# Moving small passes, splits and blank rows of an attention kernel between engines

## The reference, cut to what matters

```python
x = x + attention0(layernorm(x), ctx)        # scores / sqrt(8) + position bias, mask, softmax
x = x + ffn(layernorm(x))                    # low-rank, 512 wide, gelu
x = x + attention1(layernorm(x), ctx)        # softmax without bias
x = x + moe(layernorm(x))                    # 16 experts of 64, top 8 by tanh gate, silu, one shared
```

## Time and profile before

| what | us |
|---|---|
| median of 3 runs | 200.42 (199.63 to 200.68) |
| profiled execution, its own time | 201.42 |
| its span | 199.6 |
| PE busy | 169.8 (85%) |
| DVE busy | 148.3 (74%) |
| ACT busy | 133.3 (67%) |
| POOL busy | 91.1 (46%) |

### The profile page before, as it was taken

One profiled execution on the slowest core, in us unless ns is written; L12 is line 12 of the kernel. 1 busy time (PEld: TensorE's weight loads), 2 busy tenths in 40 slices (PEclk: granted clock), 3 DMA queues, 4 the chain that ended last, 5 costly groups with the idle time before them and its releaser, 6 DMA issues.

```text
span 199.6 us, 4779 instructions
## 1 busy us (share of the span) xinstructions
PE 169.8 (85%) x1609; PEld 120.5 (60%) x1609; DVE 148.3 (74%) x651; ACT 133.3 (67%) x289; POOL 91.1 (46%) x110
## 2 busy tenths in 40 slices
PE   0548269998979699989789679989999999999994
PEld 0325145667658366655656356857766767869783
DVE  5390369898588967998686979898986944989461
ACT  3265046999999879998988978572687674344120
POOL 8159999989789968964230533001010020110000
PEclk9999958999999979999999979999999999999999
DMA  5255796012323862000303302300010001000000
GB/s 134 80 116 130 176 252 140 1 39 72 92 56 97 218 211 68 13 0 4 82 6 78 82 8 62 96 8 0 2 32 2 0 5 30 0 2 0 29 1 26
DMA packets 21880, 12.22 MB, mean 61 GB/s; under 512 B 3120, under 2 KB 21232, under 8 KB 21856
## 3 DMA queue, kind: packets, MB, share of 16 engines
q1 hardware_dynamic: 19776, 10.68, 21.3%
q10 hardware_dynamic: 2080, 1.24, 2.4%
HBM read 4.98 MB, written 0.54 MB: 28 GB/s over the span
## 4 chain that ended last, share of the span: by engine, by line
PE 67%; ACT 12%; DVE 10%; issue 4%; POOL 4%; DMA 2%; SPq 1%; DVEq 0%; ACTq 0%
PE bank L460 17%; PE bank L489 10%; PE bank L403 8%; PE bank L359 6%; PE bank L374 4%; PE bank L343 3%; PE bank L439 3%; PE bank L429 3%; ACT pt L1401 3%; DVE es L887 3%; ACT xn L1349 2%; PE bank L413 2%; PE bank L476 2%; PE bank L420 2%; PE bank L349 2%
## 5 line engine op out<-in xcount | busy, mean ns | idle before, releaser
L887 DVE CUSTOM_DVE_ANT_0 es<-bank,biasq 128x128 f32<-128x128 f32 x128 | 28.1, 284 | 7.8 <-PE bank L359 7.6
L1735 POOL TENSOR_TENSOR es<-es,mx 128x512 f32<-128x512 f32 x32 | 32.7, 1044 | 0.7 <-DVE mx L887 0.6
L1713 POOL TENSOR_TENSOR rstd<-ve,half 128x2 f32<-128x2 f32 x16 | 11.2, 700 | 44.3 <-DVE ve L872 43.9
L1455 ACT ACTIVATE gth<-bank 128x256 f32<-128x256 f32 (+1 forms) x36 | 13.2, 382 | 21.8 <-PE bank L460 17.1
L403 PE MATMUL bank<-pt,va 128*32 128x128 f32 x512 | 26.1, 288 | 1.5 <-ACT pt L1401 0.8
L374 PE MATMUL bank<-ident,es 128*128 128x128 f32 x128 | 19.6, 294 | 4.7 <-ACT es L1395 4.1
L460 PE MATMUL bank<-xT,wg 128*128 128x256 f32 (+1 forms) x72 | 22.9, 399 | 0.1
L893 DVE TENSOR_REDUCE mx<-bank 128x4 f32<-128x512 f32 x32 | 20.5, 679 | 2.8 <-PE bank L359 2.7
L1395 ACT ACTIVATE es<-es 128x512 f32<-128x512 f32 x32 | 19.1, 630 | 5.1 <-POOL es L1735 5.1
L460 PE MATMUL bank<-xT,wu 128*128 128x256 f32 (+1 forms) x72 | 21.4, 379 | 0.0
L489 PE MATMUL bank<-wd,hT 128*128 128x128 f32 x128 | 21.2, 291 | 0.2 <-DVE hT L1010 0.2
(11 more groups left out here) (141 smaller groups left out, 343.1 us busy)
## 6 DMA issues: line engine op xcount, KB each, us to landing
k0st<-k0p SPq DMA_DIRECT2D x24, 64.0 KB, 2.1
k1st<-k1p SPq DMA_DIRECT2D x24, 64.0 KB, 2.1
q1st<-q1p SPq DMA_DIRECT2D x24, 64.0 KB, 2.0
q0st<-q0p SPq DMA_DIRECT2D x21, 64.0 KB, 2.1
biasq<-rel_bias_scratch SPq DMA_DIRECT2D x4, 256.0 KB, 4.5
wg<-in_wg SPq DMA_DIRECT2D x1, 544.0 KB, 6.0
wu<-in_wu SPq DMA_DIRECT2D x1, 544.0 KB, 6.3
x<-in_x SPq DMA_DIRECT2D x4, 128.0 KB, 4.5
```

The source lines that it names most:

```text
L887: ins = dve.tensor_tensor_reduce(es[:, b, h], src[:, s * SEQ:(s + 1) * SEQ], biasq[:, h], 1.0, 3.0e38, ALU.add, ALU.min, mx[:, 0, p, b, h: ...
L1455: act.activation(gth[0:rows, n % GATES], src[0:rows, 0:TOK], ACT.Silu).then_inc(nth("gth", n), 1)
L1735: pool.tensor_tensor(es[:, b, h], es[:, b, h], mx[:, 0, p, b, h].unsqueeze(2).broadcast_to([128, 4, SEQ]), ALU.subtract).then_inc(nth(f"le ...
```

## The change

Four things are done together.

1. `ve` and `nmr` of each layer norm, the four passes of `split_max` and the four of the combine split go from DVE to POOL. `nmr` is now one pass for each sequence. `split_max` and `router_parts` on POOL have the passes of before, behind waits on DVE's results and on their own.
2. The 15 splits: ACT casts part 0 from PSUM, PE adds the product of the negated identity with part 0 to the bank, ACT casts part 1, PE subtracts that, ACT casts part 2 and frees the bank. `first_rest`, `last_part` and `middle` are gone. The score's scale goes into the query weights (`scale_queries`, DVE), and DVE makes the negated identity.
3. The blank rows of q1 and k1 are filled by two transfers a stack from a small tile (`clear_rows`, SP; 12 in all), with -1 in k1, as the maxima are no longer negated.
4. All five orders and the bank numbers are new. In ACT's order the loads of weights stand behind all splits of pair 1 and ahead of the first exponential.

The core of the diff, with the first calls of PE, ACT, POOL and SP:

```diff
 
+            if first(j, p):
+                if part == 0:
+                    freed(q, f"{j}.{p}")
+                else:
+                    new(q, "q0_first", part) and q.wait_ge(sem("q0_first"), part)
+            elif part < 2:
+                new(q, f"{j}_part{part}", turn(j, p) + 1) and q.wait_ge(sem(f"{j}_part{part}"), turn(j, p) + 1)
+            else:
+                freed(q, f"{j}.{p}")
             if part == 0:
...
+        def clear_rows(q, j, i):
+
+            new(q, "blanks", 2) and q.wait_ge(sem("blanks"), 2)
+            for n in range(PRODS, DK):
+                load(q, stacks[j][i][n:128:DK], blanks[:, 1 if j == "k1" else 0].unsqueeze(1).broadcast_to([2 * DK, HALF, TOK]), f"{j}st{i}_in")
+
         def stacked(eng, j, p):
...
+            def less_part(j, p, part):
+
+                new(pe, "identb", 2) and pe.wait_ge(sem("identb"), 2)
+                new(pe, f"{j}_part{part}", turn(j, p) + 1) and pe.wait_ge(sem(f"{j}_part{part}"), turn(j, p) + 1)
+                pe.matmul(filling(f"{j}.{p}")[:, 0:TOK], minusb[:], parts[j][p % SPLITS[j]][:, part], start=False, stop=True,
+                          skip_group_check=True).then_inc(nth(f"{j}_less{part}", turn(j, p)), 1)
 
...
@@ -527,333 +549,363 @@
             rel_bias(0)
             front_turned(0, 1)
             project("q0", 0, 2)
-            project("k0", 0, 3)
-            project("k1", 0, 4)
+            project("k1", 0, 3)
+            project("k0", 0, 4)
+            less_part("k1", 0, 0)
+            less_part("k0", 0, 0)
+            less_part("k1", 0, 1)
             front_turned(1, 5)
-            project("k0", 1, 6)
-            project("q0", 1, 7)
+            less_part("k0", 0, 1)
+            project("q0", 1, 6)
+            project("k0", 1, 7)
             project("k1", 1, 0)
-            scores0(0, 0, 0, 1, 3)
-            scores0(0, 0, 2, 2, 4)
-            scores0(0, 1, 0, 5, 6)
+            less_part("q0", 1, 0)
+            less_part("k0", 1, 0)
+            less_part("q0", 1, 1)
+            less_part("k0", 1, 1)
+            scores0(0, 0, 0, 1, 2)
+            scores0(0, 0, 2, 5, 3)
+            scores0(0, 1, 0, 4, 6)
             scores0(0, 1, 2, 7, 1)
-            weights_turned(0, 0, 0, 3)
-            value_rows(0, 0, 3)
+            value_rows(0, 0, 2)
             value_rows(0, 1, 2)
-            values(0, 0, 0, 0, 3)
-            weights_turned(0, 0, 1, 2)
-            value_bias_out(4)
-            weights_turned(0, 0, 2, 5)
+            weights_turned(0, 0, 0, 2)
+            weights_turned(0, 0, 1, 5)
+            value_bias_out(2)
...
-                new(dve, f"mv{n}", 2 * p + 2) and dve.wait_ge(sem(f"mv{n}"), 2 * p + 2)
-                dve.tensor_scalar(ve[:, n, p], mv[:, n, p, :, 1], LN_EPS, None, ALU.add).then_inc(nth(f"ve{n}", p), 1)
-
-            def shift(n, p):
-
-                new(dve, f"rstd{n}", p + 1) and dve.wait_ge(sem(f"rstd{n}"), p + 1)
-                dve.scalar_tensor_tensor(nmr[:, n, p], mv[:, n, p, :, 0], -1.0, rstd[:, n, p], ALU.mult, ALU.mult).then_inc(nth(f"shift{n}", p), 1)
 
             def add_bias(p, b, c):
 
...
+            def scale_queries():
+                new(dve, "wqk_in", 16) and dve.wait_ge(sem("wqk_in"), 16)
+                for l in range(2):
+                    dve.tensor_scalar(wqk[:, l, 0], wqk[:, l, 0], SCALE if l else -SCALE, None, ALU.mult).then_inc(nth("wq_scaled", l), 1)
 
...
-            def evict(j, p):
+            def split(j, p, part):
 
...
-                if p >= SPLITS[j]:
+                l, to = int(j[1]), parts[j][p % SPLITS[j]][:, part]
+                if part == 0 and p >= SPLITS[j]:
                     stacked(act, j, p - SPLITS[j])
-                i = p % SPLITS[j]
-                l = int(j[1])
+                if part:
+                    new(act, f"{j}_less{part - 1}", turn(j, p) + 1) and act.wait_ge(sem(f"{j}_less{part - 1}"), turn(j, p) + 1)
                 if j[0] == "q":
                     new(act, "bqs", 2) and act.wait_ge(sem("bqs"), 2)
-                    bias, scale = bqs[:, l:l + 1], SCALE if l else -SCALE
+                    bias = bqs[:, l:l + 1]
                 else:
                     new(act, "bqk_in", 16) and act.wait_ge(sem("bqk_in"), 16)
-                    bias, scale = bqk[:, 2 * l + 1:2 * l + 2], 1.0
-                act.activation(parts[j][i][:, 0], src, ACT.Identity, bias=bias, scale=scale)
-                free(act.activation(whole[j][i][:], src, ACT.Identity, bias=bias, scale=scale), f"{j}.{p}")
-
-            def middle(j, p):
-                new(act, f"{j}_rest", turn(j, p) + 1) and act.wait_ge(sem(f"{j}_rest"), turn(j, p) + 1)
-                i = p % SPLITS[j]
-                act.activation(parts[j][i][:, 1], whole[j][i][:], ACT.Copy).then_inc(nth(f"{j}_mid", turn(j, p)), 1)
+                    bias = bqk[:, 2 * l + 1:2 * l + 2]
+                ins = act.activation(to, src, ACT.Identity, bias=bias)
+                if part < 2:
+                    ins.then_inc(nth(f"{j}_part{part}", turn(j, p)), 1)
+                else:
+                    free(ins, f"{j}.{p}")
 
...
             copy_front(0)
-            evict("k0", 0)
-            evict("k1", 0)
-            middle("k0", 0)
+            split("k1", 0, 0)
+            split("k0", 0, 0)
+            split("k1", 0, 1)
             normalize(0, 1)
-            middle("k1", 0)
             stack(act, "q0", 1, 0)
+            stack(act, "q0", 2, 0)
+            split("k0", 0, 1)
             copy_front(1)
-            stack(act, "q0", 2, 0)
-            evict("k0", 1)
-            evict("q0", 1)
-            middle("k0", 1)
-            middle("q0", 1)
+            split("k1", 0, 2)
+            split("k0", 0, 2)
+            split("q0", 1, 0)
+            split("k0", 1, 0)
+            split("q0", 1, 1)
+            split("k0", 1, 1)
+            split("q0", 1, 2)
+            split("k0", 1, 2)
+            load_wv(act)
             load_wo(act)
-            load_wv(act)
+            load_rows(act)
             load_bv(act)
             load_ffn(act)
-            load_rows(act)
             load_gate(act)
+            load_b1(act)
+            copy_values(0, 0)
             weights0(0, 0, 0)
-            load_b1(act)
             weights0(0, 0, 1)
+            copy_values(0, 1)
             copy_weights(0, 0, 0)
...
+
                 new(pool, "half", 1) and pool.wait_ge(sem("half"), 1)
+                new(pool, f"mv{n}", 2 * p + 2) and pool.wait_ge(sem(f"mv{n}"), 2 * p + 2)
+                pool.tensor_scalar(ve[:, n, p], mv[:, n, p, :, 1], LN_EPS, 1.0, ALU.add, ALU.mult).then_inc(nth(f"ve{n}", p), 1)
                 new(pool, f"ve{n}", p + 1) and pool.wait_ge(sem(f"ve{n}"), p + 1)
                 pool.tensor_tensor(rstd[:, n, p], ve[:, n, p], half[:, 0:2], ALU.pow).then_inc(nth(f"rstd{n}", p), 1)
+                new(pool, f"rstd{n}", p + 1) and pool.wait_ge(sem(f"rstd{n}"), p + 1)
+                for b in range(2):
+                    pool.tensor_scalar(nmr[:, n, p, b:b + 1], mv[:, n, p, b, 0:1], rstd[:, n, p, b:b + 1], -1.0,
+                                       ALU.mult, ALU.mult).then_inc(nth(f"shift{n}", 2 * p + b), 1)
 
             def residual(n, p):
...
+                new(pool, "nm_pads", 1) and pool.wait_ge(sem("nm_pads"), 1)
+                if p:
+                    read(pool, f"nm.{p - 1}{b}")
+                for c in range(4):
+                    freed(pool, f"S1.{p}{b}{c}")
+                to = nm[:, b]
+                src, rest = (t.rearrange("p (hh hp) -> p hh hp", hh=2) for t in (mx[:, 1, p, b], mr[:, p, b]))
+                pool.tensor_copy(to[:, 0], src).then_inc(nth(f"nm_a{b}", p), 1)
+                new(pool, f"nm_a{b}", p + 1) and pool.wait_ge(sem(f"nm_a{b}"), p + 1)
+                pool.tensor_tensor(rest, src, to[:, 0], ALU.subtract).then_inc(nth(f"nm_b{b}", p), 1)
+                new(pool, f"nm_b{b}", p + 1) and pool.wait_ge(sem(f"nm_b{b}"), p + 1)
+                pool.tensor_copy(to[:, 1], rest).then_inc(nth(f"nm_c{b}", p), 1)
+                new(pool, f"nm_c{b}", p + 1) and pool.wait_ge(sem(f"nm_c{b}"), p + 1)
+                pool.tensor_tensor(to[:, 2], rest, to[:, 1], ALU.subtract).then_inc(nth(f"nm{b}", p), 1)
+
+            def router_parts(p):
+
...
+
             def clear(j, i):
-                pool.memset(stacks[j][i][:], 1.0 if j == "k1" else 0.0).then_inc(nth(f"{j}_clear", i), 1)
+                pool.memset(stacks[j][i][:], 0.0).then_inc(nth(f"{j}_clear", i), 1)
...
             value_ones()
-            clear("q1", 0)
-            first_rest("k0", 1)
-            first_rest("q0", 1)
-            last_part("k0", 1)
-            clear("q1", 1)
-            clear("q1", 2)
+            clear_blanks()
             less_least(0, 0, 0)
             less_least(0, 0, 1)
-            last_part("q0", 1)
-            clear("k1", 0)
             less_least(0, 0, 2)
-            clear("k1", 1)
             less_least(0, 0, 3)
             less_least(0, 1, 0)
...
```

(112 more changed lines are left out.)

976 lines of the change are left out of this document (446 added, 530 removed).

## The result

The changed kernel takes 193.52 us (four runs, 192.59 to 194.42), the kernel before 200.22 (four runs beside them). The ratio is 0.967, 95% interval 0.961 to 0.972, so 6.7 us are gone. Forecast were 2.9. The profiled execution took 193.92 us, its span is 192.1.

What follows compares the result with a forecast made beforehand. TensorE, busy 169.8 of 199.6 us, bounds the kernel, with ScalarE the other full engine in the middle. Idle -5.3, clock -1.6 and products +4.0 sum to -2.9, giving 197.5 us, own range 195.5 to 199.4, whole range 193.3 to 202.8.

Steps and rivals of the forecast that it cites:

- Orders redrawn: All engine orders: fewer table loads and calls moved past the first experts, moved work counted once, priced at nothing.
- Products, +4.0: TensorE's 30 subtracting products: the 22 outside the opening at 0.18 us each cost 4.0 us, from 3.1 to 5.9.
- Middle, -5.3, and clock, -1.6: From 30 to 122 us: half of TensorE's 10.7 us idle returns, and half of 3.2 us clock loss around gaps.
- GpSimd, "no bound": GpSimd's total busy time goes from 91.1 to 87.9 us with tiny passes in and subtractions and memsets out: no bound.
- the splits' relief, "nothing": Splits in PSUM: ScalarE keeps three passes per projection at 0.48 us each, so nothing is gained.
- Opening, 0: First 30 us: hand walk to first scores at 21.3 and exponential at 27.5; nothing taken, ends -2 to +2 us.
- Tiny passes, 0.3 each: 96 tiny passes moved from VectorE to GpSimd cost 0.3 us each there, 28.8 us in all.
- rival 4: GpSimd's tiny passes cost 0.7 us each, lengthening norm and split_max chains: +4.5 us, 204.9; chance 0.07.
- Tail, nothing: From 122 to 197 us, mostly experts: TensorE idles only 0.9 us, so nothing unless its own work changes.
- Rival 3: Experts in the tail: VectorE is a hidden bound, and relief saves 3.6 us more over 36 calls: 193.9; chance 0.15.
- Rival 1: Middle, 30 to 122: ScalarE, busy 83.4 of 92 us, holds it at 92; 199.5 to 201, say 200.2; chance 0.20.
- Rival 2: At the 22 later subtracting products TensorE waits 0.4 us for ScalarE's splits: 201.9 at half, 206.3 at all; chance 0.15.

Runs made afterwards that it cites:

- e7: Kernel before with tiny passes on GpSimd and splits in PSUM, old orders but for the places of touched calls, memsets as before: 201.20 us, ratio 1.003.
- e11: Changed kernel with the router and first seven expert calls of pair 0 put back behind the scores and last queries of pairs 2 and 3: 200.25 us, ratio 0.994.
- e12: Changed kernel, same parts, all five orders drawn anew with more experts of pairs 0 and 1 ahead of 122 us: 194.25 us, ratio 0.966.
- e13: Changed kernel, same parts, a second new set of orders, nearer to the change's own: 198.29 us, ratio 0.987.
- e4: Changed kernel's orders and banks with tiny passes, splits and memsets all put back as before: 209.59 us, ratio 1.037.
- e8: Changed kernel with a second, all-zero product behind each of the 30 subtracting products: 195.01 us, ratio 0.971.
- e10: Changed kernel with 30 unconnected GpSimd passes added at the places of the old subtractions: 200.37 us, ratio 0.997.
- e2: Changed kernel with the splits back over SBUF, GpSimd subtracting in 30 passes, the 30 products gone: 202.01 us, ratio 1.003.
- e1: Changed kernel with the tiny passes back on VectorE, all else as changed: 200.85 us, ratio 0.998.
- e3: Changed kernel with blank rows of q1 and k1 cleared by six GpSimd memsets again, no blank-row transfers: 193.66 us, ratio 0.964.
- e5: Kernel before with only the tiny passes moved to GpSimd, orders otherwise as before: 203.19 us, ratio 1.014.

## Why the prediction was wrong

The direction and the place (TensorE's idle middle) were right, the size wasn't: -6.7 against -2.9. In the profiles PE's idle time fell by 9.8 us where the forecast's term had 5.3, and its busy time rose by 2.3 where its terms had 2.4 (-1.6 and +4.0). So the miss lies in the idle time. By the steps:

1. *The step that failed: "Orders redrawn", put at nothing ("moved work, counted once").* The forecast gave the whole gain of the middle to the two parts, whatever the orders. With both parts in the old orders nothing is gained: 201.20, ratio 1.003, and PE idles 10.2 us from 30 to 122 as before (e7), where the forecast, which has no term for the orders, asks for 197.5. One move of the new orders, the first experts ahead of the last scores, is worth 5.5 us with all parts unchanged (e11): it is what stands in the place where PE waited at 115. Two other orders of the same parts are 4.2 us apart (e12, e13). But the orders aren't the gain by themselves: with the old parts they lose 7.4 us against before (e4). The gain belongs to neither alone. How it divides, the runs don't tell: an undone part also leaves an order that doesn't fit it, and in the old orders I chose the places.
2. *Products, +4.0.* I divided a busy time by a count (5.9 / 32). Added a second time, thirty of them cost the kernel about 1 us (e8). With about 1 for 4 the sum would have been -5.9 and 194.5, near the result, but for the wrong reason, as 1 shows. The busy time doesn't settle what the first thirty cost: they show 0.28 to 0.31 us each, 9.0 in sum, and the engine's total rose by 2.3 while about 2 us less went to the lower clock (mean granted clock 0.964 over 199.6 us before, 0.973 over 192.1 now). Part of them must fall where PE would have stood idle.
3. *Middle, -5.3, and clock, -1.6.* 6.2 us of idle came back. That the stretch 75 to 97 can't give was right: PE idles 2.5 us there, 2.3 before. The clock loss around both gaps went whole (3.2 by the earlier trace rows), not half, but the opening ran at 0.87 against 0.92, 1.5 us more lost; the net of about 2 is near the 1.6 by that accident.
4. *GpSimd, "no bound", and the splits' relief, "nothing".* I compared totals (91.1, then 87.9) and looked at ScalarE and TensorE alone. GpSimd was busy 52.3 of 60 us between 30 and 90, with 0.7 us of idle ahead of its `less_least` calls, and I didn't read that column. In the new orders its time has a price: 19 us more of it cost 6.1 (e10), the old splits 7.3 (e2). That it held the kernel before isn't shown, and three runs speak against it, if not each by itself: relieved in the old orders it gave nothing (e7); relieved further in the new ones, the kernel was as slow as before (e1); and 9.4 us more of its busy time, by the memsets, cost nothing (e3).
5. *Opening, 0.* PE idles 2.7 us less. Its wait for the first `xn` went from 2.6 us to 0.4, and is 0.4 in e1 too, with the tiny passes on VectorE, so it isn't theirs. The walk was late at each step: first scores at 20.2 (21.3 forecast), load issues 0.49 each (0.56), exponential at 25.7 (27.5). The memsets were rightly called hidden (e3).
6. *Tiny passes, 0.3 each.* 0.20 to 0.29, 22.1 us for 96 where I had 28.8. One chain, at 64.06: `ve` to the end of `nmr` 1.6 us, of the 2.0 forecast to `xn`. Whether a dear pass (rival 4) was a danger is answered: no. The Trainium skill prefers VectorE for elementwise work and calls GpSimd slower at two inputs (GPSIMD Engine Reference, Engine selection). Pass by pass the trace agrees in direction, by less: the last pass of the combine split takes 0.24 us on GpSimd, 0.19 on VectorE. For the kernel the move cost 2.7 us in the old orders (e5), with GpSimd at 55.1 of those 60 us, and undoing it cost 6.4 in the new ones (e1).
7. *Tail, nothing.* 0.9 us of idle went. Rival 3 (193.9) named nearly the measured time, but not the cause: an expert product takes 0.38 to 0.40 us as before, and the experts start 10.6 us earlier with four score calls, a projection and pair 1's values moved behind.
8. *Rival 1, ScalarE holds the middle.* It went to 77.8 of 82 us, 95% busy, and still let the middle shorten. *Rival 2*, waits on the splits: 0.9 us in two places, both in the opening.

## What to carry to other kernels

Read an engine's load in the stretch where the bound engine idles: GpSimd was 87% busy in one and 46% in the span. Then read from the other side, who waited for it and how long. No idle time ahead of its passes means only that it has a queue; here ScalarE waited 0.4 us for that queue in the middle, and shortening it in the old orders gained nothing. A part and the order that it is put into are one change: each part alone made this kernel slower, both in the old order made it no faster, and the order without them cost 7 us. So don't price a redrawn order at nothing, and try parts and order together and apart. Price an added instruction by adding it twice, and say that this is the price of the second.

## What the runs showed that I had not expected

- Thirty products, each with 0.27 us or more of busy time in the profile, cost 0.03 to 0.04 us each when doubled (e8); their starts are 0.11 us apart.
- A plain pass on GpSimd with 1 to 32 elements a partition takes 0.20 to 0.29 us (96 of them), against 0.18 to 0.27 for these passes on VectorE before (the earlier trace rows has the first and the last).
- The adding of the mask on VectorE took 1094 ns a pass before and 672 after, for the same shape. It isn't the memsets: in e3 they are back, one add runs beside one, and it takes 0.69 us. The three slow adds of the kernel before began beside a GpSimd pass with two inputs, and each ended 0.54 us after that pass (which ended at 14.06, 26.77 and 29.51). The group after, then before, then e3:

```profile
L1074 DVE TENSOR_TENSOR biasq<-biasq,maskn 128x512 f32<-128x512 f32 x4 | 2.7, 672 | 4.0 <-DMA biasq<-rel_bias_scratch 4.0
```

```profile
26.09 0.68 POOL L1730 TENSOR_TENSOR q0p<-q0f,q0p 128x256 bf16<-128x256 f32 x1
26.11 1.20 DVE L1057 TENSOR_TENSOR biasq<-biasq,maskn 128x512 f32<-128x512 f32 x1 [4.29 <-DMA biasq<-rel_bias_scratch]
28.47 1.04 POOL L1735 TENSOR_TENSOR es<-es,mx 128x512 f32<-128x512 f32 x1
28.71 1.34 DVE L1057 TENSOR_TENSOR biasq<-biasq,maskn 128x512 f32<-128x512 f32 x1 [0.44 <-DMA biasq<-rel_bias_scratch]
```

```profile
24.28 1.81 POOL L1802 MEMSET k1st<- 128x2048 bf16 x1
25.58 0.69 DVE L1074 TENSOR_TENSOR biasq<-biasq,maskn 128x512 f32<-128x512 f32 x1 [4.26 <-DMA biasq<-rel_bias_scratch]
```

- In e11 TensorE idled 2.5 of the 10 us from 110 to 120, and the granted clock was 0.71 in 115 to 120 and 0.61 in 120 to 125; filled with expert products the same place kept 1.00.
